# Rotary cross attention: dense rows of exponentials, values turned over DRAM, one sum of heads every second slot

## The reference, cut to what matters

```python
q = (x @ Wq.T).reshape(B, T, H, D).transpose(0, 2, 1, 3)        # H = 16, D = 8, T = 128
k = (context @ Wk.T).reshape(B, S, H, D).transpose(0, 2, 1, 3)  # S = 77
v = (context @ Wv.T).reshape(B, S, H, D).transpose(0, 2, 1, 3)
q = rms_norm(q, q_norm_w)
k = rms_norm(k, k_norm_w)
q = apply_rope(q, q_cos, q_sin)
k = apply_rope(k, k_cos, k_sin)
attn = jnp.einsum('bhtd,bhsd->bhts', q, k) * scale
attn = jax.nn.softmax(attn, axis=-1)
out = jnp.einsum('bhts,bhsd->bhtd', attn, v)
return out.transpose(0, 2, 1, 3).reshape(B, T, C) @ Wo.T
...
x = _layernorm(x + _L1_xattn_ref(x, ctx_1024, ...), axis=-1)
```

## Time and profile before

| | |
|---|---|
| median of 3 runs | 2771.97 us |
| the profiled execution, its own time | 2773.75 us |
| its span in the profile | 2772.0 us |
| PE busy in the whole span | 2534.0 us (91%) |
| PE / DVE / ACT / POOL busy from 1900 to 2350 us, a part of the rotary stage | see the rows below |
| rotary stage, first transpose of x to last z | 1834.2 to 2402.7 us |

### The profile page before, as it was taken

One profiled execution on the slowest core, in us unless ns is written; L12 is line 12 of the kernel. 1 busy time (PEld: TensorE's weight loads), 2 busy tenths in 40 slices (PEclk: granted clock), 3 DMA queues, 4 the chain that ended last, 5 costly groups with the idle time before them and its releaser, 6 DMA issues. The chain is left out here.

```text
span 2772.0 us, 61590 instructions
## 1 busy us (share of the span) xinstructions
PE 2534.0 (91%) x19168; PEld 1864.5 (67%) x19168; DVE 1904.9 (69%) x5298; ACT 1671.0 (60%) x4543; POOL 1694.9 (61%) x2110
## 2 busy tenths in 40 slices
PE   8998999999999289996999999969999999699996
PEld 6665887877877289993555555547766666458993
DVE  6884677787777355555777777765788886445655
ACT  6773666666665234444766666639888887623334
POOL 3442334555555645554888888846688887724675
PEclk9998999999999699998999999979999999899998
DMA  8932467777774122214100000000011010011336
GB/s 260 338 107 68 151 215 226 234 224 224 223 220 129 54 65 71 72 58 129 58 11 9 9 11 9 7 25 13 16 30 30 30 30 17 30 30 54 93 93 194
DMA packets 274799, 267.86 MB, mean 97 GB/s; under 512 B 30060, under 2 KB 253561, under 8 KB 274096
## 3 DMA queue, kind: packets, MB, share of 16 engines
q1 hardware_dynamic: 256912, 228.42, 27.2%
q0 software_dynamic: 17280, 34.13, 3.6%
q10 hardware_dynamic: 288, 1.38, 0.2%
HBM read 101.24 MB, written 151.85 MB: 91 GB/s over the span
## 5 line engine op out<-in xcount | busy, mean ns | idle before, releaser
L779 POOL TENSOR_TENSOR wide_probs<-wide_exps,wide_inv_sum 128x616 f32<-128x616 f32 x128 | 168.3, 1315 | 305.6 <-DVE wide_inv_sum L1580 293.0
L749 POOL TENSOR_TENSOR causal_exps<-causal_biased,causal_neg_max 128x512 f32<-128x512 f32 x256 | 262.8, 1036 | 76.4 <-DVE causal_neg_max L1594 76.2
L758 POOL DMA_INDIRECT sorted_x<-send,place_i x240 | 244.1, 1017 | 84.2 <-ACT send L1233 44.0
L1289 ACT ACTIVATE rotary_exps<-banks,rotary_neg_max 128x77 f32<-128x77 f32 x1024 | 248.7, 341 | 19.3 <-DVE rotary_neg_max L1594 19.1
L1764 POOL DMA_INDIRECT results<-gelu_tile_out,gelu_dest_i x142 | 140.1, 986 | 142.2 <-DVE gelu_tile_out L1920 120.0
L1539 DVE TENSOR_TENSOR causal_biased<-banks,regions 128x512 f32<-128x512 f32 x256 | 163.6, 680 | 80.7 <-PE banks L1115 80.4
L1764 POOL DMA_INDIRECT results<-swiglu_tile_out,swiglu_dest_i x142 | 144.6, 1019 | 116.7 <-DVE swiglu_tile_out L1915 59.4
L1833 ACT ACTIVATE gelu_hidden<-banks,gelu_slot 128x256 f32<-128x256 f32 x284 | 116.6, 470 | 159.5 <-PE banks L2010 159.4
L1258 ACT ACTIVATE causal_exps<-causal_exps 128x512 f32<-128x512 f32 x256 | 161.2, 630 | 71.4 <-POOL causal_exps L749 71.4
L1594 DVE TENSOR_REDUCE rotary_neg_max<-banks 128x4 f32<-128x308 f32 x256 | 121.7, 475 | 113.5 <-PE banks L1129 105.1
L1273 ACT ACTIVATE causal_probsT<-banks 128x512 f32<-128x512 f32 x256 | 151.6, 592 | 79.3 <-PE banks L1140 79.3
(11 more groups left out here) (385 smaller groups left out, 7018.3 us busy)
## 6 DMA issues: line engine op xcount, KB each, us to landing
v_dram<-wide_staged SPq DMA_DIRECT2D x38, 1024.0 KB, 4.4
sorted_x<-blank SPq DMA_DIRECT2D x1, 34848.0 KB, 116.8
sorted_x<-blank SPq DMA_DIRECT2D x24, 1452.0 KB, 8.7
wide_folded<-v_dram SPq DMA_DIRECT2D x128, 256.0 KB
gelu_tile_in<-sorted_x SPq DMA_DIRECT2D x71, 132.0 KB, 2.1
swiglu_tile_in<-sorted_x SPq DMA_DIRECT2D x71, 132.0 KB, 2.1
gelu_back<-results SPq DMA_DIRECT2D x16, 512.0 KB, 8.0
swiglu_back<-results SPq DMA_DIRECT2D x16, 512.0 KB, 5.4
```

The lines of the kernel that those rows point to most:

```text
L749: pool.tensor_tensor(exps[:, (NU * pair.c + m) % ES], biased[:, m % BS].rearrange("p (h n) -> p h n", h=HU), neg_max[:, m % SLOTS].unsquee ...
L758: pool.indirect_dma_start(route["sorted_x"], bass.IndirectOffsetOnAxis(ap=r_place_i[:, b % 2, which, n // 2:n // 2 + 1], axis=0), send[:, ...
L779: pool.tensor_tensor(probs[:, half % SLOTS, 0:HH * NK].rearrange("p (k h) -> p h k", h=HH), exps[:, half % EB], inv_sum[:, half % SLOTS].u ...
L1289: last = act.activation(exps[:, (NU * c.c + k) % ES, h], scores[:, h * NK:(h + 1) * NK], ACT.Exp, bias=neg_max[:, k % SLOTS, h:h + 1])
```

## The change

Only the rotary kind changes in its work.

- **Exponentials** of 8 heads (two slots) go into one dense row of 616 columns, padded with zeros to 640 (5 chunks of 128). In an even slot PE transposes chunks 0 and 1, in an odd slot chunks 2, 3 and 4. ACT copies 256 and 384 columns. A row of a transposed chunk now belongs to one key of one head, and a chunk holds parts of two or three heads.
- **Values** must stand in the same order, one row for each (head, key), 616 of them for 8 heads, padded to 640. SBUF can't be turned that way by a copy, so they go over DRAM: ACT writes `v_rows` (77 keys, 32 groups of 80 columns; 8 hold values and the ninth holds a one), SP stores it by 4 DMAs of 77x8 runs of 256 bytes, and loads it by 5 DMAs into `v_dense`, two buffers, runs of 256 bytes again.
- To have time for that, the projection of values moves from the late part of pair `f` to the early part of pair `e` (`EARLY = 3`, slot 7, PSUM bank 6), 4 pairs ahead. `v_rows` has one buffer: ACT waits for the stores of the pair before.
- **Sums** (`dense_sum`): every second slot 8 matmuls, two for each of the four strips (chunk `strip` and chunk `strip + 1`), 128 rows each.
- `ctxT` has a ring of 4 instead of 8, with a wait for `early_done`. `run_steps` on SP has 6 stages. The ready count is 7 memsets instead of 5.

```diff
@@ SP
+            def store_values(pair):
+                sp.wait_ge(early_done, pair.count(EARLY, EARLY))
+                rows = route["v_dram"][4 * HALF_ROWS * pair.c:4 * HALF_ROWS * (pair.c + 1)].rearrange("(m h k) c -> h k m c", h=4, k=NK)
+                for h in range(4):
+                    sp.dma_start(rows[h], v_rows[0:NK].rearrange("k (m r) -> k m r", r=PITCH)[:, :, 64 * h:64 * h + 64]
+                                 ).then_inc(v_stored, 16)
+
+            def load_values(pair):
+                s = pair.c % 2
+                sp.wait_ge(v_stored, 16 * 4 * (pair.c + 1))
+                if pair.c >= 2:
+                    sp.wait_ge(pv_done, pair.back(2).count(NU, NU))
+                for b in range(2):
+                    for n in range(2):
+                        at = HALF_ROWS * (2 * (2 * pair.c + b) + n)
+                        sp.dma_start(v_dense[:, s, b, n, 0:4], route["v_dram"][at:at + 512].rearrange("(c p) d -> p c d", p=P)).then_inc(v_loaded[s], 16)
+                rows = route["v_dram"][2 * HALF_ROWS * 2 * pair.c:2 * HALF_ROWS * 2 * (pair.c + 1)].rearrange("(m r) d -> r m d", m=4)
+                sp.dma_start(v_dense[0:HALF_ROWS - 512, s, :, :, 4].rearrange("p b n d -> p (b n) d"), rows[512:HALF_ROWS]).then_inc(v_loaded[s], 16)
...
                 if f is not None:
                     load(f)
+                if kind == "rotary" and pair is not None:
+                    store_values(pair)
+                if kind == "rotary" and behind[2] is not None:
+                    if behind[2].c == 0:
+                        sp.wait_ge(ready, READY)
+                    load_values(behind[2])
@@ ACT, the copy of the values
-            if m == 3:
-                return act.activation(value_heads(s2)[0:NK, :, :, 0:D], f_bank[0:NK, 0:2 * P].rearrange("p (g x d) -> p g x d", g=4, x=8), copy)
+            if m == 4:
+                if f.c >= 1:
+                    act.wait_ge(v_stored, 16 * 4 * f.c)
+                return act.activation(v_rows[0:NK].rearrange("p (m w) -> p m w", w=PITCH // 4)[:, :, 0:D],
+                                      chip.banks[0:NK, 6, 0:2 * P].rearrange("p (m d) -> p m d", d=D), copy)
@@ when
-        EARLY_AT = [(0, 0), (1, 0)]
-        LATE = (2, 3)
+        EARLY_AT = [(0, 0), (1, 0), (7, 0)]
+        EARLY_PARTS = (0, 1, 4)
+        LATE = (2,)
@@ PE
+            def dense_sum(pair, n):
+                b, g, s = n // UB, n // 2 % 2, pair.c % 2
+                pe.wait_ge(probsT_done, pair.count(NU, n + 1))
+                if n == 1:
+                    pe.wait_ge(v_loaded[s], 16 * 5 * (pair.c // 2 + 1))
+                if n % UB == 1 and pair.back(1).real:
+                    pe.wait_ge(o_done, pair.back(1).count(2, b + 1))
+                for second in range(2):
+                    for strip in range(4):
+                        chunk = strip + second
+                        last = pe.matmul(o_bank[b][32 * strip:32 * strip + 32, g * P:(g + 1) * P],
+                                         v_dense[:, s, b, g, chunk, 32 * (strip % 2):32 * (strip % 2) + 32],
+                                         probsT[:, (NU * pair.c + n) // 2 % 2, chunk * P:(chunk + 1) * P], start=second == 0, stop=second == 1)
+                last.then_inc(pv_done, 2)
...
-                        for h in range(HU):
-                            last = pe.transpose(p_bank[n % 2][0:NK, h * P:(h + 1) * P], exps[:, (NU * pair.c + n) % ES, h], ident)
+                            for m in range(3 if n % 2 else 2):
+                                at = (2 * (n % 2) + m) * P
+                                last = pe.transpose(p_bank[n % 2][:, m * P:(m + 1) * P], exps[:, (NU * pair.c + n) // 2 % 2, at:at + P], ident)
```

More of the change, by code:

```diff
@@ L534, in softmax_attention @@
         ready, prepared, prepared_ps, product_done = (sem(n) for n in ("ready", "prepared", "prepared_ps", "product_done"))
-        READY = {"wide": 4, "causal": 5, "rotary": 5}[kind]
+        READY = {"wide": 4, "causal": 5, "rotary": 7}[kind]
         ROOT = 3 + 3 * NEWTON
         PREPARED = {"wide": 2, "causal": 4, "rotary": 10}[kind]
+        if kind == "rotary":
+            v_stored, v_loaded = sem("v_stored"), [sem(f"v_loaded{n}") for n in range(2)]
         if kind == "wide":
@@ L848, in front_pe @@
                     pe.matmul(f_bank[:, 2 * b * P:(2 * b + 1) * P], xT[:, s2, b], w["wq"], start=True, stop=True)
[L849 to L850 removed]
+                    last = pe.matmul(f_bank[:, (2 * b + 1) * P:(2 * b + 2) * P], ctxT[:, f.c % CTX, b], w["wk"], start=True, stop=True)
+            elif m == 4:
+                f_bank = chip.banks[:, 6]
                 for b in range(2):
[L852 removed]
+                    last = pe.matmul(f_bank[0:NK, b * P:(b + 1) * P], ctxT[:, f.c % CTX, b, 0:NK], w["wv"], start=True, stop=True)
             else:
@@ L1150, in step @@
                         weighted_sum(*at)
-                    if at is not None and late:
+                    if at is not None and kind == "causal":
                         late_sum(*at)
+                    if at is not None and kind == "rotary" and at[1] % 2 == 1:
+                        dense_sum(*at)
                     if f is not None:
@@ L1269, in step @@
                         act.wait_ge(probsT_ps, pair.count(NU, n + 1))
-                        if before(pair, n, 2) is not None:
-                            bc, bk = before(pair, n, 2)
-                            act.wait_ge(pv_done, bc.count(NU, bk + 1))
-                        act.activation(probsT[0:NK, n % 2], p_bank[n % 2][0:NK], ACT.Copy).then_inc(probsT_done, 1)
+                        if kind == "rotary":
+                            half = (NU * pair.c + n) // 2
+                            if half >= 2:
+                                act.wait_ge(pv_done, 2 * half - 2)
+                            start, columns = 2 * (n % 2) * P, (3 if n % 2 else 2) * P
+                            act.activation(probsT[:, half % 2, start:start + columns], p_bank[n % 2][:, 0:columns], ACT.Copy).then_inc(probsT_done, 1)
+                        else:
+                            if before(pair, n, 2) is not None:
+                                bc, bk = before(pair, n, 2)
+                                act.wait_ge(pv_done, bc.count(NU, bk + 1))
+                            act.activation(probsT[:, n % 2], p_bank[n % 2], ACT.Copy).then_inc(probsT_done, 1)
                     if e is not None and kind == "rotary":
@@ L1284, in step @@
                         scores = s_bank[k % 2]
-                        if before(c, k, ES) is not None:
+                        half = (NU * c.c + k) // 2
+                        if kind == "rotary" and half >= 2:
+                            act.wait_ge(probsT_ps, 2 * half - 2)
+                        if kind == "causal" and before(c, k, ES) is not None:
                             bc, bk = before(c, k, ES)
@@ L1288, in step @@
                         for h in range(HU):
-                            last = act.activation(exps[:, (NU * c.c + k) % ES, h], scores[:, h * NK:(h + 1) * NK], ACT.Exp,
-                                                  bias=neg_max[:, k % SLOTS, h:h + 1])
+                            at = (HU * (k % 2) + h) * NK
+                            into = exps[:, half % 2, at:at + NK] if kind == "rotary" else exps[:, (NU * c.c + k) % ES, h]
+                            last = act.activation(into, scores[:, h * NK:(h + 1) * NK], ACT.Exp, bias=neg_max[:, k % SLOTS, h:h + 1])
                         last.then_inc(exps_done, 1)
```

73 lines of the change are left out of this document (48 added, 25 removed).

## The result

The changed kernel takes 2754.41 us, median of 6 runs (2746.91 to 2758.86), beside 2769.97 us for the kernel before, median of 6 (2765.75 to 2773.22). The ratio is 0.9943, 95% interval 0.9925 to 0.9960: faster by 16 us. The forecast was a gain of 35 us and 2737 us. The time lies in the range given, but less than half of the gain came. The profiled execution of the changed kernel took 2758.86 us, its span 2757.0.

A forecast was written before the change was run, and what follows sets the result against it. PE mostly bounds the kernel, DVE the first routed pair. From 2773.75 us, 41.0 and 1.5 gained, 7.0 + 0.5 lost at the start: 2738.8, by the median 2737; own range 2728 to 2748, 8 in 10 2716 to 2770.

The forecast's parts named there:

- What bounds the kernel now: Stage's pace: PE in pairs without routing, 15.7 us a pair; with routing DVE the first, the others mostly PE.
- Transposes, sums, copies: Per pair: PE's transposes 1.3 us less, PE's sums 1.1 less, ACT's copies 1.4 less busy.
- The round of four: In PE's sums, a further round of four records adds 0.14 us; a block of 16 takes 0.83.
- the two terms: On PE: transposes 1.3 us and sums 1.1 us less; its work falls from 15.7 to 13.3 a pair.
- What is next, pairs without routing: PE at 13.3 and ACT at 12.8 wait for each other: 13.8 us a pair, 1.9 less.
- What is next, routed pairs: POOL next, first pair DVE's: gains 0.5, 1.8, 1.4 and 1.1 us, 4.8 a block of four.
- Values over DRAM: DMA stores and loads of values: steady loop hidden with slack 2.9 us; start 7 us later.
- the drain: DMA stores of values: landing takes 1.6 us fixed plus a drain taken as 5.3; a turn 7.3.
- The rule on 11 engines: DMA stores run on 11 engines, 6.5 us at 29 ns; start costs 12 us instead of 7, sum 2742.
- The first: POOL and DVE hold routed pairs, ACT the others: 1.2 us a pair, 2 a block; 2758; chance 0.13.
- Rivals 2, 3 and 4: 2: PE alone sets pace, 2719, 0.10; 3: store loop decides, 2764 to 2824, 0.22; 4: sums don't overlap, 2751, 0.10.

The follow-up runs named there:

- a_nodma: Changed kernel with values neither stored to DRAM nor loaded (128 stores, 160 loads left out; v_dense holds ones); ratio to the kernel before 0.9932 (0.9914-0.9951).

## Why the prediction was wrong

- **What bounds the kernel now.** Right for the pairs without routing, PE. For the routed pairs it was half right: it read DVE's 17.53 us as work, and the third pair as mostly PE's. Both were in part the scatters (2.4 us of DVE's busy time, 1.1 us of the third pair).
- **Transposes, sums, copies.** Their sizes held: 20 transposes a pair at 0.11, a block at 0.58 where 0.62 was said to show it right, copies 461 ns where the mean of 0.37 and 0.49 is 0.43. The round of four was 0.105 and not 0.14. PE's busy time fell by 1.95 us a pair where the two terms make 2.4, but that is a matter of counting: PE now stands still four times a pair, and a block's record runs 0.16 us longer before a gap (three transposes 0.49 where the next block starts after 0.33). By this estimate PE's work is 13.1 us a pair, a little under the 13.3 forecast.
- **What is next, pairs without routing.** 13.8 forecast, 14.4 measured: the allowance of 0.5 us for PE and ACT waiting for each other was too small, and no run shows what would have given the right one. Each such pair lacks 0.6.
- **What is next, routed pairs: the step that failed.** "I take 15.4, 15.3 and 14.7 for them, and for the first 17.8", 4.8 a block; measured 15.8, 16.6, 15.2 and 18.55, 1.9 a block. Without scatters it is 4.0. The step named POOL as next with 14 us of work, and then gave the pairs 0.9 to 1.2 us beyond it, as if its queue could be filled so far. Some of POOL's scatters wait for ACT or PE (29.5 us of waits between 1910 and 2334), and the keys stand behind them; 14.3 us of work took 15.2 us in the fourth pair and 16.6 in the third. And it took a gain of 0.5 from the first pair, with DVE's 17.53 us as work of its own: that pair lost 0.3 with scatters and gained 1.0 without. In these two pairs, the third and the first, the scatters took the gain. What is missing without scatters too, 0.6, 0.4 and 0.3 us in the second, third and fourth pair, stays open.
- **Values over DRAM.** The steady loop is hidden, as forecast. At the start the drain counted from the last issue was 5.3 us in the sum; the turn of 5.6 makes it 3.6, as the first stores drain while the last are issued. The sum took 7.5 us off for the start and 3.0 were lost, only 1.0 of them by the transfers. It put the longer early part itself at nothing; a_nodma shows a turn of 4.9 and 2.0 us lost without any transfer. So the size was too large and the cause for the most part another.
- **The rule on 11 engines.** The record of the first turn has 48 increments of the stores' semaphore for four stores, 11 and one more for each, which agrees with the rule of the Trainium skill (DMA: Bandwidth & Descriptors, Why a DMA increments its semaphore by 16 and not by 1) that each engine used adds one and the issuing sequencer adds the rest at once. The price worked out from it, 12 us at the start, was wrong, since 29 ns a packet was: 2724 packets in the 5.3 us of the turn kept 16 engines 64.7% busy, 20 ns each.
- **Rivals.** The first came nearest, in number (2758, 2 us a block and 1.2 a pair, measured 1.9 and 1.26) and in the mechanism of the routed pairs, which POOL and DVE hold. Its other half, that ACT holds the pairs without routing, is not borne out: less work for ACT gave 0.04 us. It had 13 chances in 100. It was set aside because the fourth pair ran at 15.8 with PE full; but that pair says only that POOL can do 13.8 us of work in 15.8, nothing of less. Rivals 2, 3 and 4 are refuted: PE stands idle in every pair, no copy waits in the steady part, the rounds overlap.
- **Luck.** That 2754 lies in the range of 2716 to 2770 is no merit of the forecast's sum: its own range of 2728 to 2748 is missed, and the value lies in the part that was added for the rivals.

## What to carry to other kernels

When an engine at 90% or more loses work, look at the in-order queue of the next engine and follow its chain with all its waits, not its busy sum: here 14.3 us of POOL's work filled 15.2 to 16.6. Busy time can hold waiting: where an instruction beside POOL lasts 0.6 us and elsewhere 0.2, the engine's share is not its work. One run with the suspected next engine relieved, in the kernel before and after, tells what a change is worth with and without that bound. And a start or a stage is measured from its own first instruction: the first transpose of the rotary stage lies between 1830.7 and 1836.0 us in the traces of kernels that don't differ before it.

## What the runs showed of the hardware

- A scatter of 128 rows of 528 bytes costs 1.0 us on POOL's queue. DVE's copies, scalar operations and two-input operations between SBUF tiles that start 0.36 us or more into it end only behind it (55 of 55 of three kinds in two traces; a few plain TENSOR_TENSORs were not held); those that start in its first 0.31 us are not held. Reductions of DVE from the banks keep their length (477 ns with scatters, 475 without).
- Such waiting is in the profile's busy time: DVE's busy time in the first pair of a block is 17.78 us with scatters and 14.88 without.
- Stores of 256-byte pieces from 77 partitions: 2464 packets in four issues of 0.55 us landed 5.1 us after the first issue (start of the changed kernel's stage), and the traffic (104 GB/s where there was 15) moved no steady period by over 0.03 us.
- The first pair of a block sometimes takes 20.4 us instead of 18.55, in the same program; runs of one kernel differ by up to 13 us (2764.19 to 2777.61 for the kernel before on one chip), so single runs can't tell a change of 5.
